# Attention over row tiles: the next tile's eleven transposes moved to the tile's beginning, the router's strips into a bank of their own

## The reference, cut to what matters

```python
x = x + _L0_gnn_ref(_layernorm(x), adj, W, a1, a2)      # x: 1354 x 512
x = x + _L0_ffn_ref(_layernorm(x), Wr, br, W1, b1, W2, b2)

def _L0_gnn_ref(input, adj, W, a1, a2):
    h = input @ W
    e = leaky_relu(h @ a1 + (h @ a2).T, 0.2)
    attention = softmax(where(adj > 0, e, -9e15), axis=1)
    return relu(attention @ h)

def _L0_ffn_ref(inputs, Wr, br, W1, b1, W2, b2):        # 8 experts, one per token
    probs = softmax(x @ Wr + br)
    # each token goes to its best expert, at most N // 8 tokens to an expert
    # eo = relu(expert_in @ W1 + b1) @ W2 + b2, scaled by the gate
```

## Time and profile before

| | |
|---|---|
| median of 3 runs | 258.79 us (258.31 to 259.61) |
| the profiled execution's own time | 259.62 us |
| its span, first to last instruction on the core | 257.9 us |
| PE (matmul) busy | 245.2 us, 95% |
| PE weight loads (PEld) busy | 207.9 us, 81% |
| DVE busy | 188.8 us, 73% |
| ACT busy | 134.2 us, 52% |
| POOL busy | 87.5 us, 34% |
| the attention's products L1492, 310 recorded in three groups | 43.2 + 41.8 + 39.0 us |
| chain that ended last, PE's share | 77% |

### The profile page before, as it was taken

The page is one execution under the profiler, slowest core; times in us unless marked ns, Lnnn a source line. Parts: engine busy times, 40 slices in busy tenths (PEclk is TensorE's granted clock), DMA queues, the critical chain, the costliest instruction groups (busy, mean ns, idle before and its releaser), DMA issues.

```text
span 257.9 us, 4589 instructions
## 1 busy us (share of the span) xinstructions
PE 245.2 (95%) x1625; PEld 207.9 (81%) x1625; DVE 188.8 (73%) x451; ACT 134.2 (52%) x289; POOL 87.5 (34%) x114
## 2 busy tenths in 40 slices
PE   6699999999999899999999999999999999999991
PEld 2389989988888687787787889899978978879880
DVE  4797848997889989988973563866486965974950
ACT  2556785884665865766672320342265364473430
POOL 4234783000124413441330224108463354321532
PEclk9999999999999999999999999999999999999999
DMA  6991000023347778731212204044998899887101
GB/s 169 370 318 70 1 4 1 11 99 108 108 151 200 232 307 287 231 135 58 82 41 84 83 0 138 13 155 128 346 300 244 265 307 297 272 316 243 53 7 44
DMA packets 19210, 40.47 MB, mean 157 GB/s; under 512 B 2810, under 2 KB 3130, under 8 KB 19188
## 3 DMA queue, kind: packets, MB, share of 16 engines
q1 hardware_dynamic: 16196, 34.17, 40.6%
q0 software_dynamic: 2176, 4.80, 5.6%
q10 hardware_dynamic: 816, 1.21, 1.5%
HBM read 32.93 MB, written 8.31 MB: 160 GB/s over the span
## 4 chain that ended last, share of the span: by engine, by line
PE 77%; DVE 8%; ACT 4%; issue 3%; POOL 3%; DMA 3%; POOLq 0%; ACTq 0%
PE bank L1492 21%; PE bank L1758 13%; PE bank L1796 7%; PE bank L1425 6%; PE bank L1823 5%; PE bank L1473 4%; PE bank L1506 3%; DMA w_raw<-in_L_gnn_W_dram 3%; PE bank L1407 2%; PE bank L1744 2%; PE bank L1771 2%; DVE adj_s L922 2%; PE bank L1518 1%; PE bank L1625 1%; DVE adj_s L944 1%
## 5 line engine op out<-in xcount | busy, mean ns | idle before, releaser
L1492 PE MATMUL bank<-h_hi,pt_hi 128*128 128x512 f32 (+1 forms) x110 | 43.2, 393 | 0.0
L1492 PE MATMUL bank<-h_hi,pt_lo 128*128 128x512 f32 x100 | 41.8, 418 | 0.0
L1492 PE MATMUL bank<-h_lo,pt_hi 128*128 128x512 f32 x100 | 39.0, 390 | 0.0
L428 POOL TENSOR_TENSOR x_all<-x_all,w_raw 128x512 f32<-128x512 f32 x10 | 21.2, 2123 | 50.4 <-ACT w_raw L617 46.7
L1758 PE MATMUL bank<-prob,w 128*128 128x168 f32 x224 | 33.2, 306 | 0.1
L1758 PEld LDWEIGHTS bank<-prob,w 128*128 128x128 f32 x224 | 32.6, 189 | 0.8 <-issue 0.3
L789 ACT ACTIVATE adj_s<-bank,b_cols 128x168 f32<-128x168 f32 x28 | 9.7, 397 | 31.3 <-PE bank L1758 31.3
L1492 PEld LDWEIGHTS bank<-h_hi,pt_hi 128*128 128x128 f32 (+1 forms) x110 | 20.6, 188 | 4.8
L640 ACT ACTIVATE wide<-adj_s,off_b 128x1354 f32<-128x1354 f32 (+1 forms) x11 | 15.7, 1431 | 12.2 <-DVE off_b L937 12.2
L1492 PEld LDWEIGHTS bank<-h_lo,pt_hi 128*128 128x128 f32 x100 | 18.9, 189 | 3.1
L1492 PEld LDWEIGHTS bank<-h_hi,pt_lo 128*128 128x128 f32 x100 | 18.8, 188 | 3.0
(11 more groups left out here) (227 smaller groups left out, 572.9 us busy)
## 6 DMA issues: line engine op xcount, KB each, us to landing
w<-in_L_ffn_W_dram SPq DMA_DIRECT2D x16, 1024.0 KB
adj_s<-in_adj_dram SPq DMA_DIRECT2D x10, 677.0 KB, 5.4
x_rows<-x_all SPq DMA_DIRECT2D x10, 257.0 KB, 3.4
out_dram<-x_all SPq DMA_DIRECT2D x10, 256.0 KB
x_all<-in_x_dram SPq DMA_DIRECT2D x9, 256.0 KB, 6.8
prob<-in_L_ffn_b_dram SPq DMA_DIRECT2D x5, 256.0 KB
w_raw<-in_L_gnn_W_dram ACTq DMA_DIRECT2D x4, 256.0 KB, 6.5
adj_s<-in_L_ffn_b_dram SPq DMA_DIRECT2D x2, 256.0 KB, 7.4
```

Source lines behind the costliest of these rows:

```text
L428: pool.tensor_tensor(x_all[0:R, t, 0:D], x_all[0:R, t, 0:D], relu_s[0:R, :], ALU.add).then_inc(s_x1, 1)
L1492: ins = pe.matmul(o_ps[par][0:R, :], p[0:K, par, k, 0:R], h[0:K, k, :], start=(k == 0 and n == 0), stop=(k == NT - 1 and n == 1))
```

## The change

It moves `p_turn(t+1, 0..2)` to the beginning of tile t, ahead of all products of the tile. The strips go to bank 0 (`strip_ps`), and `x2_turn` no longer waits for the copy of the strips. Strips, their sum and x1's transposes now stand together after the tile's last product, so that 32 products follow each other in a run. STRIPS goes from 7 to 5, and the strips and sums sit one tile later: tiles 1 to 5 go by strips, tile 6 now by a full `logits`. On ACT, `p_high(t+1, 2)` moves ahead of `low_slope(t+3)`. On DVE, `p_low(t+1, 2)` moves from the head of loop t+1 to the end of loop t, ahead of `stats2`. POOL's `residual` loses its wait for `p_low`. DVE's `biased` calls move with the strips.

```diff
-    STRIPS = 7
+    STRIPS = 5
...
+        strip_ps = banks[0][:, 0:P]
...
             def residual(t):
                 R = rows(t)
                 pool.wait_ge(s_relu, t + 1)
-                if t < NT - 2:
-                    pool.wait_ge(s_plo[2], t + 2)
...
-                act.activation(lt[:, :], x2_ps[:, 0:P], ACT.Copy).then_inc(s_lt, 1)
+                act.activation(lt[:, :], strip_ps, ACT.Copy).then_inc(s_lt, 1)
...
                 p_high(t + 1, 1 - par, 1)
-                if 3 <= t < STRIPS + 2:
-                    strip_copy(t - 2)
+                p_high(t + 1, 1 - par, 2)
+                if 4 <= t < STRIPS + 4:
+                    strip_copy(t - 3)
                 if t + 3 < NT:
                     low_slope(t + 3)
                 if t == NT - 2:
                     exp_below(0)
-                p_high(t + 1, 1 - par, 2)
...
             dve.wait_ge(s_small, 32)
+            p_low(1, 1, 2)
             for t in range(1, NT - 1):
                 par = t % 2
-                p_low(t, par, 2)
                 if t + 2 < NT:
                     argument(t + 2)
                 p_low(t + 1, 1 - par, 0)
-                if 4 <= t < STRIPS + 3:
+                if t == 3:
+                    biased(0)
+                if 5 <= t < STRIPS + 4:
+                    biased(t - 4)
+                if t == STRIPS + 4:
                     biased(t - 3)
                 sum_inverse(t + 1, 1 - par)
...
                 p_low(t + 1, 1 - par, 1)
+                p_low(t + 1, 1 - par, 2)
+                if t == STRIPS + 3:
+                    biased(t - 3)
                 if t + 3 < NT:
                     stats2(t - 1, 1 - par)
                     variance2(t - 1, 1 - par)
-                if t == 2:
-                    biased(0)
...
-            p_low(NT - 1, 0, 2)
...
             def x2_turn(t, par):
                 R = rows(t)
                 pe.wait_ge(s_x1, t + 1)
                 after(pe, s_x2, t, 1)
-                if 2 <= t <= STRIPS:
-                    pe.wait_ge(s_lt, t - 1)
...
             for t in range(2, NT - 1):
                 par = t % 2
-                p_turn(t + 1, 1 - par, 0)
+                for b in range(3):
+                    p_turn(t + 1, 1 - par, b)
                 attend(t, par, 0)
-                if 2 < t < STRIPS + 2:
-                    logit_strips(t - 2, par)
-                elif t > 2:
+                if t == NT - 2:
                     logits(t - 2, par)
-                p_turn(t + 1, 1 - par, 1)
                 attend(t, par, 1)
+                if t == NT - 2:
+                    positions(0)
+                if t == STRIPS + 3:
+                    logit_sum(t - 3)
+                attend(t, par, 2)
                 if t == 2:
                     logits(0, 0)
-                elif t < STRIPS + 2:
-                    logit_sum(t - 2)
-                if t == NT - 2:
-                    positions(0)
-                p_turn(t + 1, 1 - par, 2)
-                attend(t, par, 2)
+                if 4 <= t < STRIPS + 3:
+                    logit_sum(t - 3)
+                if 3 <= t < STRIPS + 3:
+                    logit_strips(t - 2, par)
+                if t == STRIPS + 3:
+                    logits(t - 2, par)
                 x2_turn(t - 1, 1 - par)
```

More of the change, by code:

```diff
@@ L1537, in logit_strips @@
                 for c in range(KC):
-                    ins = pe.matmul(x2_ps[c * WR:(c + 1) * WR, 0:P], wr_p[:, c, :], x2t[:, par, c, :],
+                    ins = pe.matmul(strip_ps[c * WR:(c + 1) * WR, :], wr_p[:, c, :], x2t[:, par, c, :],
                                     start=True, stop=True, tile_position=(0, c * WR))
```

## The result

The changed kernel took **261.75 us** in the median of its first 3 executions (260.12 to 263.17) against 258.79: ratio 1.0103, 95% interval 1.0059 to 1.0147. Run again beside the experiments it took 262.44 (261.29 to 264.70, 7 runs) against 258.99: ratio 1.0137 (1.0108 to 1.0165). It is slower by about 1.2%, more than the forecast of 260.0, and near the 262.0 of the rival in which the clock falls.

The account below looks back on a forecast made before the run. PE's time per tile and its waits for late DVE in tiles 2 and 3 bound the kernel. First two tiles +1.2, tiles 4 to 7 -0.35, tile 8 +0.3: +1.2 us rounded, 260.0 against 258.79; range 258.6 to 262.2.

Parts of the forecast that it names:

- the rival in which the clock falls: Tile 2's hole: PE drops to the 1.2 GHz level for some 4 us, losing 2 us, total 262.0; chance 0.16.
- Steps 1 and 2: PE, each tile: 32 products in a run save 0.16 us; eleven transposes together cost 0.12 more.
- Step 3: PE, tile's end: entering and leaving strips and sum stay nearly; half of 0.10 us saved, ends nothing and all.
- Step 4: Tiles 4 to 7 take 9.62 us each, 0.09 less, 0.35 less in all; between 0.1 and 0.8.
- Step 5: Tile 6's logits as a full product at tile 8's end: tile 8 10.00 us, 0.3 more; tile 9 nothing.
- Step 6: Tile 2's head: tile 3's transposes wait for DVE's p_low(2, 1) and p_low(2, 2); tile takes 12.50 us, +2.62.
- Step 7: Tile 3: no second hole, x1's copy wait of 1.02 goes; 9.50 us against 10.89, -1.39.
- The rival of a second hole: Tile 3's transposes: DVE slowed over 1 us, PE waits again for up to a microsecond; 261.0, chance 0.10.
- Step 8: POOL's residual, its wait removed, starts up to a microsecond earlier; cost taken: nothing.
- Step 9: ACT and DVE: group 2's p_high and p_low come earlier; batch 0's places end some 0.7 us later, covered.
- Step 10: After tile 9: nothing changed, PE on the chain; what is lost ahead reaches the end in full.
- Cheap long transposes: Rival, tiles 3 to 9: long runs at short runs' pace, eleven in 1.02 us; 1.2 gained, 258.8, chance 0.17.

Follow-up runs that it names:

- e9: Changed kernel with p_turn's groups 1 and 2 back in their old places in tiles 2 to 7; 257.81 us, ratio 0.9953 to the kernel before.
- e6: Changed kernel with p_turn's groups 1 and 2 back in their old places in all tiles; 264.53 us, ratio 1.0190 to the kernel before.
- e1: Changed kernel with 8 unused filler matmuls in tile 2's hole, between p_turn(3, 0) and p_turn(3, 1); 260.08 us, ratio 1.0044 to the kernel before.
- e2: Changed kernel with p_turn's groups 1 and 2 back in their old places in tile 2 alone; 259.28 us, ratio 1.0015 to the kernel before.
- e4: Kernel before with only ACT's and DVE's moves of p_high and p_low of group 2; 263.21 us, ratio 1.0136 to the kernel before.
- e10: Changed kernel with 17 unused transposes of a constant in tile 2's hole; 259.62 us, ratio 1.0023 to the kernel before.
- the three filled kernels: Changed kernel with tile 2's hole filled by 8 matmuls (e1), 17 transposes (e10) or 3 matmuls (e11); ratios 1.0044, 1.0023 and 1.0030.
- e3: Changed kernel with p_turn's groups 1 and 2 back between the products in tiles 2 and 3; 257.92 us, ratio 0.9945 to the kernel before.
- e11: Changed kernel with 3 unused filler matmuls in tile 2's hole; 260.00 us, ratio 1.0030 to the kernel before.
- e8: Changed kernel run again as it is, for a second profile and more times; 262.44 us, ratio 1.0137 to the kernel before.

## Why the prediction was right or wrong

- *Steps 1 and 2 (32 products, eleven transposes).* The eleven took 1.12, to the hundredth. The products took 7.37 instead of 7.44, since a further one cost 0.228, not 0.230. e9 beside the changed kernel isolates both steps: 0.09 a tile where I had 0.16 - 0.12 = 0.04. The direction was right, the size half.
- *Step 3 (strips and sum at the end).* Entering cost 0.07 (0.21 for 0.14) and leaving 0.06 (0.49 for 0.43): by these rows 0.02 of the old 0.15 is saved. In e6, which keeps all transposes in their old places, tiles 4 to 7 at 9.65 in the mean show 0.05 less than before. What I took, 0.05, is between the ends.
- *Step 4.* 9.56 for 9.62. Right, 0.06 too high.
- *Step 5.* 10.04 for 10.00, and nothing in tile 9 (9.79 for 9.75). Right.
- *Step 6 (the hole).* Idle 2.20 and 0.19 at the lines and by the releasers named, where I had 2.1 and 0.6: the profile counts idle time from the modelled end of the four transposes (0.63), I counted from their pace. From start to start the second and third group are 0.82 apart, for 0.95. The tile takes 12.55 us once the clock is held up (e1), for 12.50. Right in place, cause and size. What failed is that PE's pace behind the hole was taken as unchanged: products followed at 0.43 us up to 80.64, and the tile took 14.04.
- *Step 7 (tile 3).* 9.43 for 9.50, no wait at the strips, no second hole. The rival of a second hole is out; e2 shows it appears, with 0.99 us, only once tile 2 is mended.
- *Step 8 (POOL).* Nothing on the path, as taken. But `residual(1)` did not start earlier: it began at 80.84, with the later start 1.3 us after its 78.54 before, see below.
- *Step 9 (group 2 on ACT and DVE).* Covered, with 0.76 us to spare at the dispatch. The reason given, though, was incomplete: it is covered only because the transposes of tile 10 stand at tile 9's head. e4 shows the price without that: 1.6 us of waiting and a clock fall.
- *Step 10.* 102.2 us from `x2_turn(9)` to the end in both. Right.
- *The rival of the clock* is what happened, and it had a chance of 0.16. So the measured 261.75 fell inside the stated range by the rival that the range took in, not by the forecast's own sum. I let the 3.2 us that the trace of before survived speak against it (its clock does read 1.00 there, in windows that the cited rows don't show). Its mechanism, place and reading (0.50 in 78 to 80 us) were right; its price of 2 us was 1.5, as the slow stretch lasted about 3.4 us and part of that passed in waiting and in the three transposes. The warm-up matmuls were a weak source for that price, since the profile's granted clock reads 1.00 there although they go at half the pace; the products at 0.43 us with 0.50 granted now show it. Two things were wrong in the weighing. The one trace was one draw: its clock survived 1.74 and 0.78 us idle, while the changed kernel's trace lost it at the same place of the program with only 1.12 and 0.77 us idle. And the text named transposes without products as the danger, which e10 refutes: idle time is. The hole has 2.39 us of it, about as much as that pause of before (2.52); with the outcome of that pause not fixed, the rival should have been a close one instead of 0.16.
- *Cheap long transposes*: refuted, 102 ns each in each run of eleven.

The forecast's sum of +1.2 in the stretch is confirmed by the three filled kernels (+1.02 and +1.03), so it was 0.2 too high, mostly because tiles 3 to 7 came out 0.04 to 0.07 shorter each. The other 1.5 of the +2.53 is the clock.

## What to carry to other kernels

Moving consumers to the head of a period takes the cover from whoever feeds them: price the first periods, where the feeder is still catching up, one by one, and leave these in the old order (e3: 0.9945 where the whole change gave 1.0137). An idle time of 2 us on TensorE may cost more than half as much again through its clock (here 1.5 us); three matmuls on a free bank, some 0.7 us, were enough against it here, and 17 transposes did as well. Moves on different engines may need each other: ACT's and DVE's without PE's cost 4 us here (e4; PE's without theirs was not run). Look at what the reordered engine has in its queue behind the moved wait.

## What the runs showed of the hardware

- Transposes alone, 32 in 4.4 us with 0.55 us idle among them, kept the granted clock at 1.00 (e10).
- A waiting PE lost the clock after 2.20 us idle (two profiles) and after the 1.6 us at the dispatch (e4, e6), but not after 1.55 + 0.19 in e11 nor 0.99 in e2. In each case the fall came behind the wait, when the engine was at work again: 0.6 us behind it in the changed kernel, 1.7 in e8, 2.6 in e4. Idle time alone does not decide it: the trace before survived 1.74 and 0.78 us, the changed kernel's lost its clock in that very place with 1.12 and 0.77 (a line of PE's waits, and one of its timeline):

```profile
PE bank L1397 <- ACT w L508: 1.1, 1, 1.1
...
12.73 3.68 PE L1410 MATMUL bank<-w_raw,x2t 128*128 128x256 f32 x8 [0.77 <-ACT x2t L517]
```

- POOL's one-element `power2` took 0.55 us in all calls in the trace before but one (0.61). In the changed kernel six calls took 1.86 or 1.87. Each of the six began 0.15 or 0.16 us after a DVE L943 had begun, and ended 0.4 after that one's end. The call at 87.66, which began 0.01 us after an L943, took 0.55; the four that met none took 0.55 to 0.61. So `residual(1)`, freed of its semaphore, still began only at 80.84. POOL's timeline in the changed kernel, and DVE's L943 beside the first and the last of its lines:

```profile
79.00 1.86 POOL L432 TENSOR_TENSOR x_all<-ve,half 128x1 f32<-128x1 f32 x1 [5.73 <-DVE ve L987]
80.84 1.09 POOL L427 TENSOR_TENSOR x_all<-x_all,w_raw 128x512 f32<-128x512 f32 x1
87.66 0.55 POOL L432 TENSOR_TENSOR x_all<-ve,half 128x1 f32<-128x1 f32 x1 [5.73 <-DVE ve L987]
...
78.84 1.62 DVE L943 SCALAR_TENSOR_TENSOR adj_s<-adj_s,off_a,wide 128x1354 f32<-128x1354 f32 x1
...
87.65 1.63 DVE L943 SCALAR_TENSOR_TENSOR adj_s<-adj_s,off_a,wide 128x1354 f32<-128x1354 f32 x1
```

The page's group of this line in the changed kernel (busy time and mean ns of one over its 11 calls; before the mean was 554 ns):

```profile
L432 POOL TENSOR_TENSOR x_all<-ve,half 128x1 f32<-128x1 f32 (+1 forms) x11 | 14.0, 1271 | 53.8 <-DVE ve L987 53.8
```

That the two engines hinder one another there is read from the times only; no run took it apart.
